# The shift rows' transfers moved from the ScalarE queue to the SyncE queue of a cross-attention and mixture-attention kernel, with all places of its calendar searched anew

## What is computed

```python
x = x + xattn(layernorm(x), ctx, ctx, lens, Wq, Wk, Wv, Wo)   # softmax(q k^T / sqrt(32), masked) v, then Wo
h = layernorm(x)
top_vals, top_idx = top_k(relu(h.mean(1) @ gw1.T + gb1) @ gw2.T + gb2, 2); gates = softmax(top_vals)
q, k, v = (_svd_moe(h, p, top_idx, gates) for p in "qkv")     # 16 heads of 32
x = x + _svd_moe(softmax(q k^T) v, "o", top_idx, gates)
```

## Time and profile before

| | before |
|---|---|
| median of 3 runs | 1422.72 us |
| span of the profiled execution, first to last instruction | 1426.7 us |
| PE busy | 1391.0 us, 97% of the span, 5704 matmul records |
| DVE, ACT, POOL busy | 951.9, 861.3, 679.8 us |
| DMA queue of SP / of ACT | 128.55 MB / 1.17 MB |

### The profile page before, as it was taken

How to read it: one execution, slowest core, us unless ns; L and a number is a source line. 1 busy time by engine, 2 the same in 40 slices (tenths; PEclk the granted TensorE clock), 3 DMA queues, 4 the chain that set the end, 5 groups by cost and what they waited for, 6 DMA issues and landing times.

```text
span 1426.7 us, 17122 instructions
## 1 busy us (share of the span) xinstructions
PE 1391.0 (97%) x5704; PEld 702.4 (49%) x5704; DVE 951.9 (67%) x1687; ACT 861.3 (60%) x1499; POOL 679.8 (48%) x411
## 2 busy tenths in 40 slices
PE   8998999999999999999999999999999999999987
PEld 5545444545455444555555445455545454444432
DVE  4454577766767677767777677767777677666572
ACT  2425474866577663975658664876648665565652
POOL 2011143545555362556445463555625455465675
PEclk9889999999999999999999999999999999999999
DMA  7514233522434224522234224332235323233210
GB/s 252 143 53 133 46 68 96 153 76 46 98 110 108 75 54 125 137 61 76 68 111 123 75 59 135 110 85 67 58 104 152 76 46 97 64 101 79 81 39 30
DMA packets 78767, 130.81 MB, mean 92 GB/s; under 512 B 26374, under 2 KB 32134, under 8 KB 75607
## 3 DMA queue, kind: packets, MB, share of 16 engines
q1 hardware_dynamic: 74007, 128.55, 33.4%
q10 hardware_dynamic: 4672, 1.17, 0.4%
HBM read 66.08 MB, written 12.21 MB: 55 GB/s over the span
## 4 chain that ended last, share of the span: by engine, by line
PE 85%; ACT 7%; issue 2%; DMA 2%; POOL 2%; DVE 1%; ACTq 0%; SPq 0%; POOLq 0%
PE pj L1217 43%; PE scT L1302 9%; PE sc L1274 8%; PE acc L1331 7%; PE sc L1263 4%; PE pj L1247 2%; PE pj L1311 2%; PE scT L1295 2%; PE pj L1319 2%; PE pj L1340 2%; DMA qs<-shift 2%; PE pj L1190 1%; ACT xhat L810 1%; PE pj L1202 1%; PE pj L1211 1%
## 5 line engine op out<-in xcount | busy, mean ns | idle before, releaser
L925 ACT ACTIVATE probs<-scT 128x512 f32<-128x512 f32 x512 | 288.9, 594 | 303.9 <-PE scT L1302 300.8
L1048 DVE TENSOR_REDUCE negmax<-sc 128x1 f32<-128x512 f32 x512 | 338.0, 684 | 140.7 <-PE sc L1274 139.7
L784 POOL TENSOR_TENSOR probs_sum<-probs_sum,probs 128x1024 f32<-128x1024 f32 x128 | 300.2, 2365 | 57.4 <-ACT probs L925 57.3
L1075 DVE RECIPROCAL inv_sum<-pj 128x128 f32<-128x128 f32 x256 | 225.0, 921 | 59.9 <-PE pj L1340 39.2
L1274 PE MATMUL sc<-ks,qs 96*128 96x512 f32 x512 | 260.1, 541 | 2.4 <-DVE negmax L1048 1.6
L1217 PE MATMUL pj<-XT,Wqk 128*128 128x512 f32 x512 | 257.3, 598 | 0.6 <-DVE Wqk L1140 0.6
L1302 PE MATMUL scT<-qs,ks 99*128 99x512 f32 x512 | 250.9, 517 | 6.2 <-DMA qs<-shift 3.2
L780 POOL TENSOR_TENSOR probs_sum<-probs 128x1024 f32<-128x1024 f32 x64 | 151.4, 2372 | 173.8 <-ACT probs L925 173.8
L790 POOL TENSOR_TENSOR uv_stack<-UVS_sb,uv_stack 96x1024 fp32r<-96x1024 f32 x32 | 75.7, 2367 | 178.1 <-ACT UVS_sb L832 178.1
L1302 PEld LDWEIGHTS scT<-qs,ks 99*128 99x128 f32 x512 | 94.7, 191 | 124.5 <-ACT probs L925 60.4
L754 POOL TENSOR_TENSOR xhat<-xhat,inv_sum 128x128 f32<-128x128 f32 (+1 forms) x56 | 45.1, 806 | 207.7 <-DVE inv_sum L1075 207.7
(11 more groups left out here) (103 smaller groups left out, 1716.6 us busy)
## 6 DMA issues: line engine op xcount, KB each, us to landing
Wqk<-in_WmT SPq DMA_DIRECT2D x16, 1024.0 KB, 6.1
Wvo<-in_WmT SPq DMA_DIRECT2D x16, 1024.0 KB, 6.5
UVS_sb<-in_UVS SPq DMA_DIRECT2D x64, 192.8 KB, 3.4
qs<-stage_lo SPq DMA_DIRECT2D x136, 64.0 KB, 2.2
qs<-qs SPq DMA_DIRECT2D x34, 256.0 KB, 3.0
X<-in_x SPq DMA_DIRECT2D x8, 1024.0 KB, 6.0
ks<-stage_lo SPq DMA_DIRECT2D x128, 64.0 KB, 2.0
ks<-ks SPq DMA_DIRECT2D x32, 256.0 KB, 3.0
```

The source lines that it names most:

```text
L784: nc.gpsimd.tensor_tensor(probs_sum[:, pair], probs_sum[:, pair], probs[:, kt % 2, pair], ALU.add)\
L925: nc.scalar.activation(probs[:, kt % 2, jj, :], scT[:, ST[step], :], ACT.Exp, scale=SCALE)\
L1048: nc.vector.tensor_reduce(negmax[:, 0, n:n + 1], sc[:, SC[step], :], AX.X, ALU.max, negate=True)\
L1075: nc.vector.reciprocal(inv_sum[:, INV[use], at], pj[:, PJ[left_in(full)], at])\
```

## The change

The two transfers of `move_shift` are begun by SP, at their place in the same list of steps, through SP's DMA queue; ACT no longer has the steps `shift_move` and `cross_shift_move`. All numbers of `CALENDAR` and `OWN` are new (their unit is 16 times finer), so that the order of the instructions differs on all five engines. What each instruction does and how often it runs is the same: 3908 matmul instructions on either side.

```diff
-PERIOD = 2034
+PERIOD = 32544
 CALENDAR = {
-    "shift": (1339, 1901, 2375, 2899),
-    "shift_move": (1367, 1967, 2390, 2987),
+    "shift": (21567, 30781, 38378, 46050),
+    "shift_move": (22340, 31488, 38543, 46215),
...
@@ block.sync
+            def move_shift(side, dst, done, b, turn):
+                for part, split in enumerate(("shift_hi", "shift_lo")):
+                    sp.wait_ge(split, sp.after(split, *turn))
+                    row = SHIFT_ROW + part
+                    queue.dma_start(dst[row:row + 1].rearrange("p j (t n) -> p (j t) n", n=P).bitcast(F32),
+                                    shift[side * SIDE:side * SIDE + HJ * TT, part, :].bitcast(F32)).then_inc(sems[done], 16)
...
-                     "residual2": residual2})
+                     "residual2": residual2, "shift_move": shift_move,
+                     "cross_shift_move": cross_shift_move})
@@ block.scalar
-            def move_shift(side, dst, done, b, turn):
-                for part, split in enumerate(("shift_hi", "shift_lo")):
-                    act.wait_ge(split, act.after(split, *turn))
...
-                      "q1_rows": q1_rows, "qk_rows": qk_rows, "shift_move": shift_move, "cross_shift_move": cross_shift_move, "csT": csT, "sT": sT,
+                      "q1_rows": q1_rows, "qk_rows": qk_rows, "csT": csT, "sT": sT,
```

More of the change, by code:

```diff
@@ new lines @@
+    "context": (-28312,),
+    "context_v": (-23830,),
+    "load": (-34483,),
+    "stats": (-30774, -30622, -30591, -30572),
+    "deviation": (-30119, 1124),
+    "normalize": (-28648, 1847),
+    "xpose": (-27861, -27841, -27360, -27305, 1988, 2090, 3092, 3203),
+    "q1": (-26513, -26478, -26384, -26328, -26203, -25843, -25621, -25086, -15614, -15388, -14363, -13493, -11773,
+        -11355, -11341, -10944),
+    "q1_split": (-25877, -23662, -13154, -9945),
+    "q1_rows": (-25190, -17967, -12626, -7269),
@@ L104 @@
+    "accout": (33397, 38870, 47541, 55469),
+    "den": (29441, 38068, 47210, 55010),
+    "inv": (29801, 30080, 30251, 30735, 38225, 38584, 38610, 38800, 47410, 47507, 47639, 47669, 55166, 55500, 55643,
+        55939),
+    "divide": (38965, 44013, 52853, 56796, 56916, 57149, 57799),
+    "out2": (56207, 56343, 56736, 56806, 59616, 60391, 60506, 61339, 60048, 60412, 61131, 61427, 62272, 62601, 62795,
+        62850),
+    "residual2": (57504, 61348, 62407, 62943),
 }
 OWN = {
-    "context_keys": {(0, 0): -11084, (1, 0): -10576, (2, 0): -9150, (3, 0): -8881, (0, 1): -8717, (1, 1): -8570,
-        (2, 1): -1258, (3, 1): -1209},
@@ new lines @@
+    "context": {(0,): -77506},
+    "context_v": {(0,): -31805, (7,): 203794},
+    "wm_load": {(7, 3): 322464, (0, 0): 3910, (0, 1): 4882, (0, 2): 6713, (7, 1): 234401, (7, 0): 233015,
+        (7, 2): 228994},
+    "uv_load": {(7, 3): 242116, (0, 0): 5273, (0, 1): 5401, (0, 2): 7447, (7, 2): 236218, (7, 0): 232451,
+        (7, 1): 232523},
+    "uv_hi": {(7, 3): 285878, (0, 0): 5527, (0, 1): 8206, (0, 2): 10768, (7, 1): 235995, (7, 2): 238449,
+        (7, 0): 233022},
+    "uv_lo": {(7, 3): 290648, (0, 0): 6197, (0, 1): 8665, (0, 2): 11117, (7, 1): 236076, (7, 2): 238944,
+        (7, 0): 233920},
@@ L255 @@
+    "mask": {(): -348663},
+    "key_rows": {(0,): -352948, (1,): -153138},
 }
@@ L894, in qk_rows @@
                                          ACT.Copy).then_inc(sems["rows_copied"], 1)
-            def move_shift(side, dst, done, b, turn):
-                for part, split in enumerate(("shift_hi", "shift_lo")):
-                    act.wait_ge(split, act.after(split, *turn))
-                    row = SHIFT_ROW + part
-                    queue.dma_start(dst[row:row + 1].rearrange("p j (t n) -> p (j t) n", n=P).bitcast(F32),
-                                    shift[side * SIDE:side * SIDE + HJ * TT, part, :].bitcast(F32)).then_inc(sems[done], 16)
-            def shift_move(step, b, j):
-                move_shift(0, qs[:, slot_of(j)], "shift_moved", b, ("shift", b, j))
-            def cross_shift_move(step, b, i):
-                move_shift(1, cross_stack(b, i), "cross_shift_moved", b, ("cross_shift", b, i))
             def csT(step, b, i, j):
```

145 lines of the change are left out of this document (90 added, 55 removed), and 206 rows, old and new, of tables (CALENDAR, OWN).

## The result

The changed kernel takes 1472.85 us (median of 4 runs, 1471.11 to 1474.09) against 1422.62 us for the kernel before in the same comparison: a ratio of 1.034 with a 95% interval of 1.0302 to 1.0379, 50 us slower. The forecast was 1418 us in a range of 1403 to 1432.

The account below looks back on a forecast made before the run. PE's own pace was taken to bound the middle. The terms -10.2 - 3.2 + 1.8 + 9.3 - 2 = -4.3 us gave a span of 1422.4, less 4.0 for the profiled run: 1418 us, range 1403 to 1432.

Parts of the forecast that it names:

- What bounds the kernel: PE's own pace bounds the middle (busy 1391.0 of 1426.7 us); the start and tail are bound by chains between engines.
- Column groups, -10.2 us: On PE, 33 fewer unbroken runs of column groups (144 to 111), at 0.31 us each, save 10.2 us.
- the third rival: Matmuls between column groups were needed to cover ACT's exponentials; PE waits for probs, the 10.2 us gain falls away: 1428, chance 0.10.
- PE's busy time, which was to fall by some 10 us: Sign in the profile after that the forecast is right: PE busy some 10 us less.
- The old waits for the rows, -3.2 us: All six PE waits for the shift rows, 3.2 us over the whole span, may go: -3.2 us (0 to -3.2).
- Job 2, +1.8 us: Job 2's rows stand behind a 1 MB weight load on SP; 0.3 us of wait in six periods: +1.8 us.
- Job 1 behind the load of X, +9.3 us: Job 1's rows land just after X on SP's queue; PE waits 1.7 us in five periods, 0.8 in batch 0.
- the second rival: Waits for X in the middle periods also take PE's clock down, making the kernel slower: about 1434 us, chance 0.13.
- That a queue of its own passes the load by: Small transfers on ACT's own queue pass a 1 MB load of SP, read from 8 KB transfers landing in 2.0 us.
- The start, -2 us: First 105 us: the load of weights now stands behind batch 0's shift rows: -2 us (0 to -4.5).
- I price them at nothing, within 6 us either way: All other waits of the start and tail, in new places, count as 0, within 6 us either way.

Follow-up runs that it names:

- The split kernel: e7 with seven column groups of a period moved behind the next other matmul, 155 runs of column groups instead of 111; 1445.9 us.
- e7: Changed kernel with hiddenB by a reduction, the load of X behind job 1's shift rows, and job 0's first score later; 1427.6 us.
- e8: e7 with, at the last gate, the turning of job 2 of batch 6 two column groups earlier and the Wqk load behind its rows; 1428.2 us.
- e10: e8 with the load of Wqk for the last batch ahead of SP's wait for that batch's gate; 1423.4 us.
- e5: Kernel before with the shift rows begun by SP, those of job 2 placed behind the two stack copies of job 3; 1433.6 us.
- e12: e5 with hiddenB by a reduction and two more places mended where SP stood at rows DVE had not split; 1422.4 us.
- The four combinations: Old order with rows begun by ACT 1422.6 us, by SP 1471.0; new order with rows begun by ACT 1521.5, by SP 1472.9.
- e1_shift_on_act: Changed kernel with the shift rows begun by ACT again, all new calendar numbers kept; 1521.5 us.

## Why the prediction was wrong, point by point

**What bounds the kernel: right, and used for one wait only.** PE's own pace bounds the middle. From that the prediction concluded for the rows of job 1 that nothing pays a wait back. The same holds for every other new wait: where PE is hardly ever idle, each wait of 1 or 2 us is paid in full in every period, and in some of them once more by the clock.

**Column groups, -10.2 us: the price is right, the gain did not come.** The split kernel shows the price. But between the second and the last gate the changed kernel has 26 runs fewer, 8 us by that price, and no such gain is seen: PE's idle time there rose from 7.1 to 29.3 us and the half clock cost at most about 20, together some 42 us; the six periods are 41.3 us longer, so little is left for a gain of 8. The two stretches, before and after:

```profile
253.97:1238.61 984.64, 977.54 (x4139) 494.32 (x4138) 696.28 (x1235) 642.31 (x1123) 506.07 (x302) 1.00 0.34 90
```

```profile
251.84:1277.77 1025.93, 996.63 (x4141) 503.60 (x4141) 703.32 (x1236) 632.09 (x1122) 503.13 (x299) 0.98 0.33 86
```

With the waits mended, three profiles of the new order (e7, e8, e10) give middle periods of 163.2 to 163.9 us; the old order gives 163.9 on ACT and 163.3 to 163.4 on SP (e5 and e12). The four runs fewer in a period should have saved 1.2 us. Where this went stays open; it was not by waits for `probs`, as the third rival had it (1.8 us in four waits, 2.9 in five before). PE's busy time, which was to fall by some 10 us as a sign of being right, rose from 1391.0 to 1400.5 us, stretches at half clock included.

**The old waits for the rows, -3.2 us: right** for the middle. In e5, where the old order has the rows on SP and one number differs, none is left in the six periods, and these are 3.3 us shorter (984.6 to 981.3). In the new order with the load moved a single one of 0.36 us is left there.

**Job 2, +1.8 us: too high.** Begun 5.0 to 5.9 us after the load of Wqk, when that load had landed or nearly so, the rows landed after 1.8 to 2.0 us, and PE did not wait for them in the middle.

**Job 1 behind the load of X, +9.3 us: right in mechanism and place, the waits right in size, the price too low.** Five waits of 1.7 to 2.7 us, 10.2 us; the later of the two rows lands 0.35 to 0.55 us behind X. In batch 0, where I had put 0.8 us, there was none. But taking the waits away gave back 20.3 us. What was left out of the term is mainly the clock: behind three of the five waits (2.25, 2.65, 1.86 us) it fell for 3.4 us each. That is the second rival, which I had priced for six waits of 2.4 us and given 0.13; it came true at three of them. That a queue of its own passes the load by, as I read from the earlier trace rows, is wrong too (last section); the earlier trace rows, 4.3 us on ACT's queue beside a load of SP, pointed the other way.

**The start, -2 us: not shown.** It is 2.1 to 2.4 us shorter at the first two gates, but three kernels that are alike up to there (e7, e8, e10) reach the first gate at 116.2, 113.1 and 115.7 us: the runs differ by more than the term, and that the number fits is luck.

**The step that failed** is that the sum has no term for new waits in the middle other than those for the shift rows. Its only price for waits in new places, "I price them at nothing, within 6 us either way", is said of the start and the tail; for the six middle periods such waits are put at nothing without a word. `hiddenB` alone was worth 20.8 us: 10.0 us of waits and a fall of the clock in each of the six periods and at the last gate. The cause is the order: in the kernel before POOL is idle at the gate (from 579.24 to 580.65, while `hiddenB` runs from 580.41 to 580.69), in the new one it is in a stretch of 7 us of additions. The prediction read neither DVE's row nor POOL's place, though the trace of before had the warning: seven times 0.28 us and once 1.33, in the last batch, where a POOL addition from 1236.03 to 1238.38 was running and `hiddenB` ended at 1238.47. The Trainium skill (SBUF — State Buffer, section Who interferes with whom) has the rule: a `tensor_scalar` of VectorE can take the port pair that it shares with GpSimd, whoever comes first holds it for the whole instruction, and "the other **fully blocks**", while a `tensor_reduce` does not contend. This case agrees with both halves: 2.09 us beside a running addition for the one, 0.29 us for the other. By that rule the order of POOL at each gate would have had to be read in the new list.

The rest of what was missed: 0.9 to 1.2 us for `qs<-qs` in every period, because the copies of the `ks` rows stand ahead of those of the `qs` rows on ACT and SP and PE asks 1 us too early (6.8 us in seven waits), and the place behind the last gate, where the load of the weights and the rows of job 2 were brought so close that 7.1 us of waiting stand in one place.

**The frame was wrong too.** The change was weighed as a move of two transfers plus a better order of PE's rows. The four combinations show that queue and order cannot be priced apart: a transfer on an engine that works its list in order brings its wait with it, and what is queued behind that wait must be moved as well. Freed of their waits, the old order on either queue and the new order on SP come to the same 1422 to 1423 us.

## What to carry to other kernels

When a transfer moves to another engine's queue, look first at what stands behind it in that engine's list: the engine stands at the transfer's wait, and here one such row cost 37 us until it was moved behind two others. Where one engine is busy 97% of the time, every change of order must be followed wait by wait on all engines, since nothing there is "priced at nothing"; the spread of a row's durations (277/279/1331 ns) was the sign here of an instruction that depends on what another engine happens to do. A float32 `tensor_scalar` on DVE beside long additions of POOL can be worth writing in a form that does not wait for them: 20.8 us in the new order, nothing in the old one, where it met an addition only once.

## What the runs showed of the hardware that was not expected

**A small transfer did not pass a large one on another engine's queue.** The prediction read the 2.0 us of an 8 KB pair on ACT's queue beside a load of SP as passing it. In the kernel with the rows on ACT, a pair was begun 0.46 us behind a 1 MB load of SP:

```profile
328.77 0.41 SPq L728 DMA_DIRECT2D Wvo<-in_WmT  x1
329.23 0.51 ACTq L966 DMA_DIRECT2D qsc<-shift  x1
329.78 0.60 ACTq L966 DMA_DIRECT2D qsc<-shift  x1
```

```profile
Wvo<-in_WmT SPq DMA_DIRECT2D x1, 1024.0 KB, 5.2
qsc<-shift ACTq DMA_DIRECT2D x2, 8.0 KB, 4.7
```

It took 4.7 us and landed with the load, as the rows on SP's own queue landed with X; in this kernel five pairs stand so, at 4.6 to 4.9 us each, where a pair with no load near it takes 1.8. The row cannot tell: begun about 3.5 us after a load that took 5.4, the pair had 1.9 us of that load ahead of it, and landed after 2.0, hardly more than alone. The Trainium skill (DMA: Bandwidth & Descriptors, section Issuing engines are not separate DMA queues) says that transfers begun by different engines run on the same DMA engines and interleave; the 4.7 us agree. That a DMA engine takes turns between the queues, as the Trainium skill has it (DMA: Bandwidth & Descriptors, section Queues, rings and completion order), did not bring the small transfer through sooner here.

Rows can be late, too, with no large load begun ahead of them. In the kernel before, the rows of job 2 on ACT's queue at 592.20 us took 3.3 and 3.6 us, while SP began the experts at 592.56 and Wqk at 593.69; on SP's own queue, ahead of the same loads (at 592.43 in e5), they took 2.6 and 2.4 us. Whether the queue makes this difference, or that SP then begins the loads about a microsecond later, was not separated.

**The length of a wait does not decide alone whether the clock falls.** Behind 1.53 us at the gate it fell in every middle period, to 1.2 GHz for 3.4 to 6.8 us; behind 2.25 us for the rows in the kernel with the reduction it did not, and behind waits of 1.86 and 2.65 us in the changed kernel it did. Ahead of the wait at the gate PE runs four matmuls of one column each (L1374), ahead of the others products and scores of 512; without a wait the gate leaves the clock alone. But the work ahead does not decide alone either: at the same place, the `sT` of job 1, the clock stayed at 2.4 GHz behind 1.81 us (568.44) and fell behind 1.86 us (1082.40) in the changed kernel, and in e1_shift_on_act it stayed behind 3.02 us (763.36) and fell behind 3.08 us (939.43). What decides stays open.
